# A decoder layer whose experts run in 32 units by half of the batch, with the routing moved into the parts around it

## The reference

```
u = x @ B.T ; h = scan over the row axis, h[l] = A * h[l-1] + u[l] ; x = LN(x + h @ W.T + b)
q = x @ Wq.T + bq ; k, v likewise from ctx ; rotary on q, k ; 16 heads of 16
p = softmax(q k^T / 4 where |i - j| <= 50, else -1e9) ; x = LN(x + (p v) @ Wo.T + bo)
probs = softmax over the rows of silu(x @ router_w1) @ router_w2        16 experts
weights, idx = top_k(probs, 64)  per sequence and expert ; weights = weights / (sum(weights) + 1e-9)
for each expert e: y = (silu(x[idx] @ w1[e]) * (x[idx] @ w2[e])) @ w3[e] * weights
x = LN(x + y added at the rows idx)
```

## Time and profile before

| | us |
|---|---|
| median of 3 runs (1187.45 to 1188.78) | 1187.57 |
| the profiled execution, own time | 1182.92 |
| its span, first to last instruction | 1181.1 |
| PE busy | 1036.4 (88%) |
| DVE, ACT, POOL busy | 665.4, 534.9, 667.2 |
| mean granted TensorE clock | 0.955 |

### The profile page before, as it was taken

The page is one execution under the profiler, slowest core; times in us unless marked ns, Lnnn a source line. Parts: engine busy times, 40 slices in busy tenths (PEclk is TensorE's granted clock), DMA queues, the critical chain, the costliest instruction groups (busy, mean ns, idle before and its releaser), DMA issues.

```text
span 1181.1 us, 22568 instructions
## 1 busy us (share of the span) xinstructions
PE 1036.4 (88%) x6564; PEld 874.2 (74%) x6564; DVE 665.4 (56%) x2184; ACT 534.9 (45%) x1179; POOL 667.2 (56%) x808
## 2 busy tenths in 40 slices
PE   4689999999999998740799999999999999999980
PEld 3568877778787876430588888888888888888880
DVE  4577777777777776317444454344544444544427
ACT  1255555555455555420444554444545445545431
POOL 5456665666566665411536566566565565565453
PEclk8899999999999999875799999999999999999995
DMA  5333333333333222041335453455453454544348
GB/s 157 101 99 92 94 98 101 86 107 98 91 90 90 72 64 65 19 152 58 117 93 112 110 119 58 107 120 103 110 105 68 111 115 107 115 75 94 46 79 260
DMA packets 91184, 116.89 MB, mean 99 GB/s; under 512 B 14049, under 2 KB 66402, under 8 KB 90978
## 3 DMA queue, kind: packets, MB, share of 16 engines
q1 hardware_dynamic: 64370, 81.71, 23.2%
q0 software_dynamic: 24576, 33.57, 17.2%
q10 hardware_dynamic: 2160, 0.78, 0.3%
HBM read 65.41 MB, written 29.36 MB: 80 GB/s over the span
## 4 chain that ended last, share of the span: by engine, by line
PE 41%; DVE 4%; issue 3%; ACT 2%; DMA 1%; POOL 0%; ACTq 0%; DVEq 0%; SPq 0%; POOLq 0%
PE y_bank L1124 15%; PE gate_bank L1124 12%; PE value_bank L1124 12%; PE turn_bank L1134 2%; DVE w_lo L1260 2%; ACT w_hi L1192 1%; DVE hidden L1279 1%; DMA acc_rows<-y,slots_now 1%; DVE last L1303 1%; DVE stats L1310 1%; DMA raw<-in_w 0%; DVE xT_lo L1265 0%; DVE mv L1314 0%; POOL acc_rows L1087 0%; ACT y L1217 0%
## 5 line engine op out<-in xcount | busy, mean ns | idle before, releaser
L1087 POOL DMA_INDIRECT acc_rows<-y,slots_now x128 | 209.4, 1636 | 186.6 <-ACT y L1217 164.7
L1279 DVE TENSOR_TENSOR hidden<-gate,value_bank 128x512 f32<-128x512 f32 x128 | 88.0, 687 | 253.6 <-ACT gate L1226 235.7
L731 DVE CUSTOM_DVE_ANT_0 scored<-score,band 128x178 f32<-128x178 f32 x512 | 153.1, 338 | 80.3 <-PE score L443 69.6
L605 ACT ACTIVATE probsT<-scoreT 128x356 f32<-128x356 f32 x256 | 117.8, 470 | 169.8 <-PE scoreT L471 77.9
L1226 ACT ACTIVATE gate<-gate_bank 128x512 f32<-128x512 f32 x128 | 76.6, 598 | 221.9 <-PE value_bank L1124 221.9
L1068 POOL DMA_INDIRECT rows<-x_rows,rows_now x128 | 136.8, 1069 | 60.0 <-issue 46.2
L1124 PE MATMUL y_bank<-w_hi,h_hi 128*128 128x256 f32 x512 | 146.5, 286 | 0.0
L1124 PE MATMUL y_bank<-w_hi,h_lo 128*128 128x256 f32 x512 | 144.4, 282 | 0.0
L1124 PE MATMUL y_bank<-w_lo,h_hi 128*128 128x256 f32 x512 | 144.0, 281 | 0.0
L443 PE MATMUL score<-k_stack,q_stack 96*128 96x178 f32 x512 | 123.1, 323 | 6.7 <-DMA q_stack<-low_q 4.2
L471 PE MATMUL scoreT<-q_stack,k_stack 97*128 97x356 f32 x256 | 114.8, 449 | 0.0
(11 more groups left out here) (149 smaller groups left out, 2327.2 us busy)
## 6 DMA issues: line engine op xcount, KB each, us to landing
raw<-in_w SPq DMA_DIRECT2D x48, 512.0 KB
k_stack<-high_k SPq DMA_DIRECT2D x128, 64.0 KB, 2.2
q_stack<-high_q SPq DMA_DIRECT2D x128, 64.0 KB, 2.4
xin<-in_x SPq DMA_DIRECT2D x16, 256.0 KB, 3.0
xT<-in_xT SPq DMA_DIRECT2D x16, 256.0 KB, 3.2
cT<-in_cT SPq DMA_DIRECT2D x16, 256.0 KB, 3.7
k_stack<-low_k SPq DMA_DIRECT2D x64, 64.0 KB, 2.2
q_stack<-low_q SPq DMA_DIRECT2D x64, 64.0 KB, 2.3
```

Source lines behind the costliest of these rows:

```text
L605: nc.scalar.activation(probsT[g % 2][:, u % HG, :, :].rearrange("p a s -> p (a s)"), scoreT[u % 2][:, 0:2 * SPAN], ACT.Exp, scale=1.0 / DH ...
L731: op = nc.vector.tensor_tensor_reduce(scored[t % 2][:, q, :], score[t % 2][:, q * SPAN:(q + 1) * SPAN], band[:, q, :], -1.0, BIG, ALU.add, ...
L1087: nc.gpsimd.indirect_dma_start(dram["acc"][c], bass.IndirectOffsetOnAxis(ap=slots_now[it.r % 2][:, c:c + 1], axis=0), y[m][:], None, compu ...
L1279: nc.vector.tensor_tensor(hidden[f % 2][:], gate[f % 2][:], value_bank[f % 2][:], ALU.mult).then_inc(hidden_ready, 1)
```

## The change

The expert part is a loop over 32 units: 16 experts on sequences 0 to 7 (units 0 to 15), then 16 experts on sequences 8 to 15. A unit is what a half was; `w1`, `w2`, `w3` are loaded and split in every unit, one tile at a time between the gates. Of the routing, the first group runs inside mixing: silu in step 14, logits, softmax and the eight rounds in step 16, the rest in step 17; the second group runs in units 0 to 6. The block `routing` is gone; its last steps stand in two helpers, `weigh_picked` (its L945 to L952) and `place_picked` (L964 to L966), for one group each. The first weights are loaded and the first rows gathered while mixing ends; `xT`, `cT`, `xin`, `rot` share their memory with them (`arena`). The LayerNorm of sequences 0 to 7 is done in units 18 to 30.

```diff
+def find_maximum(dve, route, logits):
+    dve.tensor_reduce(route.nmax[:], logits, AX.X, ALU.max).then_inc(route.chain, 1)
+    dve.wait_ge(route.chain, 1)
+    dve.tensor_scalar(route.nmax[:], route.nmax[:], -1.0, None, ALU.mult).then_inc(route.nmax_ready, 1)
+def scale_probabilities(dve, route):
+    dve.wait_ge(route.exp_done, 1)
+    dve.reciprocal(route.total[:], route.total[:]).then_inc(route.chain, 1)
+    dve.wait_ge(route.chain, 2)
+    dve.tensor_scalar(route.p[:], route.p[:], route.total[:, 0:1], None, ALU.mult).then_inc(route.chain, 1)
+def take_eight(dve, route, r):
+    cols = slice(8 * r, 8 * r + 8)
+    dve.wait_ge(route.chain, 3 + 2 * r)
+    dve.max(route.top[:, cols], route.p[:]).then_inc(route.chain, 1)
+    dve.wait_ge(route.chain, 4 + 2 * r)
+    dve.max_index(route.where[:, cols], route.top[:, cols], route.p[:])
+    dve.match_replace(route.p[:], route.top[:, cols], route.p[:], -1.0).then_inc(route.chain, 1)
...
-            for i in range(10, 18):
+            for i in range(10, 15):
+                step(Iter(0, i, 4))
+            sp.wait_ge(x2_kept, 16 * (NB // 2) + 1)
+            for c in range(NC2 // 2):
+                sp.dma_start(dram["acc"][c], dram["x2"][c // CB][c % CB * 2 * S:(c % CB + 1) * 2 * S, :]).then_inc(acc_set[0], 16)
+            step(Iter(0, 15, 4))
+            sp.wait_ge(ready["U"], NB)
+            sp.wait_ge(ready["V"], NB)
+            sp.wait_ge(xb_ready, NB)
+            for n, name in enumerate(("w1", "w2", "w3")):
+                sp.dma_start(keep["raw"][n], dram[name][0:1].rearrange("o (k p) f -> p (o k) f", p=P)).then_inc(raw_in[n], 16)
+            for i in (16, 17):
                 step(Iter(0, i, 4))
...
+            pool.wait_ge(route.placed, 1)
+            nc.gpsimd.tensor_copy(keep["rows_now"][0][:], keep["row_of"][:, 0, 0:NC2 // 2]).then_inc(rows_taken, 1)
+            pool.wait_ge(rows_taken, 1)
+            pool.wait_ge(x2_kept, 16 * (NB // 2) + 1)
+            for m in range(NC2 // 2):
+                nc.gpsimd.indirect_dma_start(
+                    keep["rows"][0][:, m, :], None, dram["x2"][0],
+                    bass.IndirectOffsetOnAxis(ap=keep["rows_now"][0][:, m:m + 1], axis=0)).then_inc(rows_in[0], 16)
...
+                    if it.fixed and it.i == NB and t == 3:
+                        pe.wait_ge(rw2_set, 1)
+                        pe.wait_ge(silu_done, 1)
+                        pe.wait_ge(scored_ready, NH * NB)
+                        for c in range(GB):
+                            mm = nc.tensor.matmul(score[0][:, 0:S], rw2_placed[:, c, :], r1[:, c * S:(c + 1) * S],
+                                                  start=(c == 0), stop=(c == GB - 1))
+                        mm.then_inc(logits_ready, 1)
+                    if it.fixed and it.i == NB + 1 and t == 9:
+                        pe.wait_ge(route.picked, 1)
+                        for n, src in enumerate((route.token, route.weight)):
+                            nc.tensor.transpose(scoreT[n][:, 0:P], src[:].rearrange("p a s -> p (a s)"),
+                                                ident[:]).then_inc(rows_turned, 1)
...
+                    if it.fixed and it.i == NB - 2 and t == 9:
+                        act.wait_ge(freed["R"], GB + FREED_EARLY["R"])
+                        half = r1[:, 0:GB * S]
+                        nc.scalar.activation(half, half, ACT.Silu).then_inc(silu_done, 1)
+                    if it.fixed and it.i == NB and t == 5:
+                        act.wait_ge(route.nmax_ready, 1)
+                        nc.scalar.activation(route.p[:], score[0][:, 0:S], ACT.Exp, bias=route.nmax[:, 0:1],
+                                             accum_out=route.total[:, 0:1]).then_inc(route.exp_done, 1)
...
+                    if it.fixed and it.i == NB:
+                        if t == 4:
+                            dve.wait_ge(logits_ready, 1)
+                            find_maximum(dve, route, score[0][:, 0:S])
+                        if t == 5:
+                            scale_probabilities(dve, route)
+                        if t in range(6, 14):
+                            take_eight(dve, route, t - 6)
+                    if it.fixed and it.i == NB + 1:
+                        if t == 1:
+                            weigh_picked(dve, route)
+                        if t == 10:
+                            dve.wait_ge(rows_turned, 2)
+                            dve.wait_ge(rw2_in, 48)
+                            place_picked(dve, route, keep, slice(0, NC2 // 2), scoreT)
...
+            def load(it, n):
+                sp.wait_ge(w_lo_ready[n], it.lin(1, 0))
+                src = dram[("w1", "w2", "w3")[n]][bass.ds(it.e, 1)].rearrange("o (k p) f -> p (o k) f", p=P)
+                sp.dma_start(raw[n], src).then_inc(raw_in[n], 16)
...
+            def gather(it):
+                now = rows_now[it.par]
+                if it.at_least(2):
+                    pool.wait_ge(rows_turned, it.lin(KT, -KT))
+                if it.is_unit(NE):
+                    pool.wait_ge(route.placed, 1)
+                nc.gpsimd.tensor_copy(now[:], row_of[:, bass.ds(it.e, 1), CB * it.h:CB * it.h + CB].rearrange("p o c -> p (o c)")
+                                      ).then_inc(rows_taken, 1)
+                pool.wait_ge(rows_taken, it.lin(1, 1))
+                met()
+                for m in range(CB):
+                    nc.gpsimd.indirect_dma_start(
+                        rows[it.par][:, m, :], None, dram["x2"][it.h],
+                        bass.IndirectOffsetOnAxis(ap=now[:, m:m + 1], axis=0)).then_inc(rows_in[it.par], 16)
+            def scatter(it):
+                now = slots_now[it.par]
+                nc.gpsimd.tensor_copy(now[:], slot_of[:, bass.ds(it.e, 1), CB * it.h:CB * it.h + CB].rearrange("p o c -> p (o c)")
+                                      ).then_inc(slots_taken, 1)
+                pool.wait_ge(slots_taken, it.lin(1, 1))
+                if it.is_unit(0, NE):
+                    pool.wait_ge(acc_set[it.h], 16 * CB)
+                for m in range(CB):
+                    c = CB * it.h + m
+                    if not it.is_unit(0, NE):
+                        pool.wait_ge(added[c], it.lin(16, -16 * NE * it.h))
+                    pool.wait_ge(y_scaled, it.lin(CB, m + 1))
+                    met()
+                    nc.gpsimd.indirect_dma_start(
+                        dram["acc"][c], bass.IndirectOffsetOnAxis(ap=now[:, m:m + 1], axis=0),
+                        y[m][:], None, compute_op=ALU.add).then_inc(added[c], 16)
...
+            def unit(it):
+                if it.is_unit(0):
+                    nc.gpsimd.memset(rw2_placed[:], 0.0).then_inc(rw2_zeroed, 1)
+                if has_next(it):
+                    gather(it.step(1))
+                if it.is_unit(0):
+                    pool.wait_ge(rw2_zeroed, 1)
+                    pool.wait_ge(rw2_in, 16)
+                    for c in range(GB):
+                        op = nc.gpsimd.tensor_copy(rw2_placed[:, c, c * NE:(c + 1) * NE], rw2[:])
+                    op.then_inc(rw2_set, 1)
                 if it.at_least(1):
+                    scatter(it.step(-1))
...
-            def expert(it):
-                more = not it.fixed or it.i < NE - 1
-                nxt = Iter(it.j, it.r + 1)
-                if more:
...
-                    take(nxt, rows_now, row_of, rows_taken)
-                    gather(nxt, 0)
-                if it.at_least(1):
-                    scatter(Iter(it.j, it.r - 1), 1)
-                if more:
-                    gather(nxt, 1)
-                take(it, slots_now, slot_of, slots_taken)
-                scatter(it, 0)
...
+            def unit(it):
+                up(it)
+                if has_next(it):
+                    turn(it.step(1))
+                if it.is_unit(0):
+                    pe.wait_ge(rw2_set, 1)
+                    pe.wait_ge(silu_done, 1)
+                    for c in range(GB):
+                        b = GB + c
+                        mm = nc.tensor.matmul(y_bank[0][:, 0:S], rw2_placed[:, c, :], r1[:, b * S:(b + 1) * S],
+                                              start=(c == 0), stop=(c == GB - 1))
+                    mm.then_inc(logits_ready, 1)
+                if it.is_unit(1):
+                    pe.wait_ge(logits_kept, 1)
+                if it.is_unit(6):
+                    pe.wait_ge(route.picked, 1)
+                    pe.wait_ge(y_scaled, it.lin(CB, -CB))
+                    for n, src in enumerate((route.token, route.weight)):
+                        nc.tensor.transpose(y_bank[n][:, 0:P], src[:].rearrange("p a s -> p (a s)"),
+                                            ident[:]).then_inc(picked_turned, 1)
+                    pe.wait_ge(route.placed, 1)
                 if it.at_least(1):
+                    down(it.step(-1))
...
+            def unit(it):
+                if it.is_unit(0):
+                    half = r1[:, GB * S:NB * S]
```

(55 more changed lines are left out.)

590 lines of the change are left out of this document (258 added, 332 removed).

## The result

The changed kernel takes 1343.87 us (median of 4, 1341.93 to 1346.83) against 1187.74 of the kernel before beside it (4 runs, 1187.45 to 1188.78): ratio 1.1315, 95% interval 1.129 to 1.134. It is 156 us slower. I had forecast 41 us slower, with a range up to 1266: the sign was right, the size was not, and the range didn't hold the time.

The account below looks back on a forecast made before the run. It took a closed loop through GpSimd's scatters and gathers to bound the experts at 20.3 us a unit: 550 + 649.7 + 22.5 = 1222.2, scaled to a 1229 us median, 3.5% slower; range 1176 to 1266.

Parts of the forecast that it names:

- Start, 550 forecast: Up to unit 0's first product: mixing 513.5, plus 29 growth, plus 7.5 to the first product, against 568.0 before.
- table loads: ScalarE in mixing: 26 loads of 1.28 us, partly hidden in idle time; with Silu, logits and search, mixing grows by 29.
- Units, 649.7 forecast: Unit 0's first product to PE's end: 61 + 29 x 20.3 us, against 580.3 before.
- The loop: Experts: turn, down, scatter, gather, next turn form a closed loop of 19.2 us, 20.3 with additions, over 17.96.
- scatters, take and gathers: GpSimd's part of each unit: four scatters and the take of row numbers 8.50 us, four gathers 5.02.
- landing: Last gather's rows arriving before PE's turn, in each unit: 2.0 us.
- turn to scatter: From the start of PE's turn through the first `y` group to GpSimd's first scatter: 3.7 us per unit.
- clock 0.3 counted: PE's clock falls after its stand before the turn in one unit in five: 0.3 us per unit.
- loads beside the landing 0 counted: Doubled weight loads in the units keep DMA at some 0.6 busy and cost nothing by themselves.
- DVE 0.8 counted: Weight subtractions on DVE lengthen GpSimd's scatter and gather issues: 0.8 us per unit.
- Rival D: Experts: the clock falls in nearly every unit, 1.2 us more per unit, 35 us, giving 1264; 15%.
- Tail, 22.5 forecast: After PE's end: only the last chunk's scatter, load, LayerNorm and store count, 22.5 us against 32.8 before.

Follow-up runs that it names:

- the table kept: Changed kernel with the Ln and Exp table loaded again right behind the Silu of mixing step 14: 1322.17 us.
- small subtractions: Changed kernel, but from unit 2 on each weight subtraction on DVE works on 64 columns instead of 1024: 1269.28 us.
- small loads: Changed kernel, but from unit 2 on each weight load brings 64 KB instead of 512 KB: 1281.78 us.
- where the stands are nearly filled: Changed kernel with 64 KB weight loads and 64-column subtractions from unit 2, and twelve added PE products before each turn from unit 8: 1233.30 us.
- the thirty products: Changed kernel, but from unit 8 on PE makes thirty added products while it would stand before a turn: 1309.06 us.
- both small: Changed kernel with 64 KB weight loads and 64-column weight subtractions from unit 2 on, without added products: 1244.35 us.
- Order in the kernel before with the same loop: Kernel before, with each half's gather issued one half ahead, behind the scatters, instead of two ahead: 1257.23 us, ratio 1.058.
- an edit of a few lines that restored two steps: Changed kernel with GpSimd gathering rows two units ahead instead of one: 1159.26 us, ratio 0.976 to the kernel before.

## Why the prediction was wrong

Against the span of 1222.2 that it summed, 1345.0 is 122.8 more.

- **Start, 550 forecast, 564.85 measured: 14.8 more.** 8.1 of it lie before step 14, in two loop starts of mixing with the clock down, no part of the change. The table loads were 26 at 1.28 us, as counted, and steps 14 to 17 grew by 35.9 instead of 29: the chain hid 9 us of the loads, less than I gave it. I had also left out the copy to `acc_rows` altogether; with the table kept it costs step 15 1.1 to 4.5, as a 2 KB transfer waits behind it, while in the changed kernel itself no wait of PE in that step ends with this transfer. From mixing's end to the first product 8.0 against 7.5, and I had put the end of mixing 0.6 too late. (the earlier trace rows begins at the Silu's place, 18 us into step 14, and not at its start.)
- **Units, 649.7 forecast, 753.45 measured: 103.8 more.** This is the failed step. The loop was the right mechanism, and its bare terms hold: 13.5 us for scatters, take and gathers with small subtractions (8.50 + 5.02 counted), landing 2.04 with small loads (2.0), turn to scatter 4.05 where the stands are nearly filled (3.7). Its additions were mis-sized, per unit: clock 0.3 counted, 1.7 measured (5.75 less 4.05; the thirty products alone bring 1.5); loads beside the landing 0 counted, 1.4 measured; DVE 0.8 counted, 1.3 measured; the base 0.35 more. That is 3.65, as from 20.3 to 23.97, and 29 x 3.58 = 104 by the turns.
- Why mis-sized: each was read from the kernel before, where it is rare. The landing of 2.0 is from the earlier trace rows, where the weight loads had landed already (their queue moves 0.01 MB in these 2.0 us); the weight loads then stood in every second half, and I wrote that they "cost nothing by themselves", which is true of their bandwidth (0.48 busy) and of ACT and DVE, and not of the transfer that has to land beside them. The clock I gave one unit in five, though the earlier trace rows had it down, 0.57 in the mean of four us, after a stand of 3.11, and my own loop left 2.3. What a fall costs a unit, five times my 0.3, was an estimate that no run before the result shows; the runs showed 1.5 to 1.7. The terms feed each other: subtractions and landing make the stand longer (4.30 in the mean against 2.24 with both small), the clock falls behind more of the stands (29 of 29 against 12), and that makes the next scatter late (5.75 from the turn against 4.71). Rival D named the clock and stopped at 1264, since it kept the other terms.
- **Tail, 22.5 forecast, 26.7 measured: 4.2 more.** I had let the last chunk count alone. Its scatter is issued 5.7 us after PE's end (4.7 counted), its rows are back 10.5 later (8.1, of which 3.6 for a load of 512 KB; the eight loads of the kernel before took 5.4 in the median), and DVE, which takes the four chunks one after another at 3.0 each, comes to it 2.0 us after that; from there it is 8.6 (9.3).
- **Order in the kernel before with the same loop:** 20.37 us and 1257.2, as the total of the prediction's terms says (1187.7 + 30 x 2.3 = 1257). The total fits a kernel with half the weight traffic, and that in part by luck: turn to scatter was 0.7 longer there than counted, and DVE's 0.8 didn't show. The change has all of the weight traffic.

## What to carry to other kernels

When a reordering closes a loop through a queue (consumer, producer, transfer, consumer), first count how many steps ahead the transfer is issued: an edit of a few lines that restored two steps turned 13% slower into 2% faster, though all the added work stayed. If the loop must stay closed, take each term at its loaded price, with the transfers and instructions that will run beside it, and where the sum leaves PE standing for some 2 us, price the half clock for a good part of the units: here it fell behind 11 of 23 stands that were 2.2 us in the mean (both edits), and behind all 29 of the changed kernel, of 2.4 to 5.6. And look at the built order for table loads behind a new function on ScalarE: here one Silu brought 26 of 1.28 us into mixing, and one line saved 22 us.
